# Second-order attention on one NeuronCore: the waits of a visit's state products, the bank of every other output mix, and one residual's place

## The chip, the cores and the metric

The kernel runs on one core of a Trainium2 chip. The metric is the time of one execution on the device in microseconds (us), the median of several runs. The profile is one execution taken by the hardware profiler; its rows give the busy time of TensorE (PE, with PEld for its weight loads), VectorE (DVE), ScalarE (ACT) and GpSimd (POOL).

## What is computed

Eight layers run one behind the other on an input of 8 x 1024 rows of 256 numbers, each as x = x + layer(layernorm(x)). The change touches the fifth, a second-order linear attention with 16 heads of 32 dimensions. The reference, cut to that layer:

```python
def step(carry, qkv):
    S_K, C_QV, G = carry
    q_t, k_t, v_t = qkv
    C_prev = GAMMA * C_QV
    k_C = jnp.einsum('bhk,bhkv->bhv', k_t, C_prev)
    G = GAMMA * G + k_t[..., :, None] * k_C[..., None, :]
    S_K = GAMMA * S_K + k_t[..., :, None] * k_t[..., None, :]
    C_QV = C_prev + q_t[..., :, None] * v_t[..., None, :]
    S_C = jnp.einsum('bhij,bhjv->bhiv', S_K, C_QV)
    o_t = jnp.einsum('bhk,bhkv->bhv', q_t, S_C - G)
    return ((S_K, C_QV, G), o_t)
_, outs = jax.lax.scan(step, (S_K0, C_QV0, G0), (q, k, v))
out = outs.transpose(1, 0, 2, 3).reshape(Bs, Ts, H * DV)
return out @ Wo
```

GAMMA is 0.99; q, k and v are x @ Wq, x @ Wk and x @ Wv.

## The kernel before

All layers are written by hand: each engine has its own program, in a fixed order, and waits on semaphores for the others. The layer in question is the function second_order_attention. It works in chunks: the 8192 rows are 64 tiles of 128 rows (NT = 64), eight tiles to a batch (TB = 8). The 16 heads are four groups of four (HG = 4, UT = 4), and a **visit** t is one tile with one group: t runs over 256 visits (NU), tile(t) = t // 4. Every group carries three 32x32 states per head from tile to tile of its batch. A visit *carries* a state (carries(t)) unless its tile is the first of its batch, and updates it unless its tile is the last.

PE's loop over t runs from L1792 of the listing on. One turn of it does, in this order:

- keys_queries(t) (L1651), the products of keys and queries of the chunk, into the four banks so_rows, and queries_U(t-1) (L1659). DVE masks the first (mask_AB, L1962) and the second (mask_P, L1970) into AB and PT.
- turn_KQ(t) and turn_W(t-1) (L1672, L1673, L1666), transposes into bank U. ACT copies them out as KW and KQe (L1885, L1891, L1892).
- a **filler**, which has nothing to do with the visit's own heads: by t % 8 it is a projection of v (0 and 1, L1708), of q or k (3 to 6, L1688), or a **mix**, the product with Wo of a finished tile (L1719). mixes_at(t) puts the mix of an even tile m at t = 4m + 7, so t % 8 = 7, and that of an odd tile at t % 8 = 2, followed there by turn_x (L1681), the transpose of the next tile pair's normalised x into bank J.
- the products of the visit: state_to_UW(t) (L1734 into bank U, L1737 into bank C), state_to_O(t-1) (L1743 and L1746 into bank X), keys_to_U(t) (L1752), values_to_W(t) (L1759), values_to_O(t-1) (L1766, L1769), state_products(t-1) (L1776, L1779, bank X).

Four PSUM banks are shared: U, C, X and J. Bank X holds the mix in its first 256 columns, the state updates and O behind them. Bank J holds the projections and turn_x, each copied out by ACT (copy_turned, copy_V, copy_xT) and for x also read by DVE (low_xT, L1936).

The state products work on 32x32 tiles of the array. Head h of the four sits on row group h, and its column group differs:

```python
nc.tensor.matmul(bU[head_rows(h), 0:P], state_of(t, 0, h), QTg[head_rows(h), tile(t) % 2, t % UT],
                 start=True, stop=False, tile_position=(h * DK, h * DK))
nc.tensor.matmul(bC[turned_rows(h), 0:P], state_of(t, 2, h), KTg[head_rows(h), tile(t) % 2, t % UT],
                 start=True, stop=False, tile_position=(h * DK, (h + 1) % HG * DK))
nc.tensor.matmul(bX[crossed_rows(h), O_AT], state_of(t, 2, h), Ug[head_rows(h), t % 2],
                 start=True, stop=False, tile_position=(h * DK, (h + 2) % HG * DK))
```

DVE's turn t: copy_O(t-2) (L1956), update(t-2) (L1946, L1948), mask_AB(t), mask_P(t-1), at t % 8 = 2 low_xT, then residual(m) for a mix of this turn (L1975: X = X + bank X, which also increments x_ready), and statistics of the rows one turn later (L1979). POOL multiplies by the decay (QTg, KTg, Ug) and makes the low part of O (L2041). PE waits for x_ready before anything in a visit writes bank X again.

Of the kernel before, what the change touches and what calls it, by code (L numbers as in the profile page):

```python
# [21 lines left out]
NT = BATCH * TB  # L22
# [1521 lines left out]
def second_order_attention(nc, R, A, C, joined):  # L1544
# [6 lines left out]
    with Stage(nc, "so") as st:  # L1551
# [46 lines left out]
        def mixes_to(t):  # L1598
            return sum(len(mixes_at(n)) for n in range(t + 1))
# [22 lines left out]
        with joined.stack:  # L1622
# [16 lines left out]
            def _(pe):  # L1639
# [62 lines left out]
                def project_V(i):  # L1702
                    if i % 2 == 0:
                        pe.wait_ge(s_["KT_ready"], halves_to(i))
                    else:
                        pe.wait_ge(s_["V_ready"], i)
# [5 lines left out]
                def mix(i, t):  # L1712
                    pe.wait_ge(s_["O_ready"], UT * (i + 1))
                    pe.wait_ge(s_["S_ready"], updates_to(min(t - 2, NU - 1)))
                    pe.wait_ge(s_["O_copied"], min(t - 1, NU))
                    if i >= 1:
                        pe.wait_ge(s_["x_ready"], i)
                    for m, (a, b, u) in enumerate((a, b, u) for a, b in PARTS for u in range(UT)):
                        last = nc.tensor.matmul(bX[:, 0:HID], OT[:, a, (UT * i + u) % (2 * UT)], wo[:, b, u],  # L1719
                                                start=(m == 0), stop=(m == UT * len(PARTS) - 1))  # L1720
# [8 lines left out]
                def state_to_UW(t):  # L1729
                    pe.wait_ge(s_["S_ready"], updates_to(t - UT))  # L1730
                    pe.wait_ge(s_["QTg_ready"], carrying_tiles_to(tile(t)))
                    pe.wait_ge(s_["KTg_ready"], carrying_tiles_to(tile(t)))
# [7 lines left out]
                def state_to_O(t):  # L1740
                    pe.wait_ge(s_["Ug_ready"], carries_to(t))
                    for h in range(HG):
                        nc.tensor.matmul(bX[crossed_rows(h), O_AT], state_of(t, 2, h), Ug[head_rows(h), t % 2],  # L1743
                                         start=True, stop=False, tile_position=(h * DK, (h + 2) % HG * DK))
                    for h in range(HG):
# [46 lines left out]
                for t in range(NU + 3):  # L1792
# [25 lines left out]
                    if t < NU and carries(t):  # L1818
                        state_to_UW(t)
                    if 2 <= t <= NU:  # L1820
                        pe.wait_ge(s_["O_copied"], t - 1)
                        pe.wait_ge(s_["S_ready"], updates_to(t - 2))
                        if mixes_to(t) >= 1:
                            pe.wait_ge(s_["x_ready"], mixes_to(t))
                    if 1 <= t <= NU and carries(t - 1):
                        state_to_O(t - 1)
# [97 lines left out]
            def _(dve):  # L1924
# [48 lines left out]
                def residual(i):  # L1973
                    dve.wait_ge(s_["out_done"], i + 1)
                    nc.vector.tensor_tensor(R.X[:, i, :], R.X[:, i, :], bX[:, 0:HID], ALU.add).then_inc(s_["x_ready"], 1)  # L1975
# [9 lines left out]
                for t in range(NU + 4):  # L1985
# [14 lines left out]
                    if t == STATS_AT + NT // 2 + 2:  # L2000
                        dve.wait_ge(s_["std_ready"], 2)
                        scales(nc, c, R, REST)
                        nc.vector.memset(R.turnstile[:], 0.0).then_inc(s_["scaled"], 1)
                    if 1 <= t <= NU:
# [3 lines left out]
                    for m in mixes_at(t):  # L2008
                        residual(m)
# [1210 lines left out]
```

## Time and profile before

| | us |
|---|---|
| median of 3 runs (lowest, highest) | 3633.62 (3632.8, 3638.25) |
| the profiled execution's own time | 3635.29 |
| its span in the profile | 3633.3 |
| the loop over the visits, from 1523.6 to 2812.95 | 1289.4 |

The profile's timeline rows begin with the start of a group of instructions and how long it lasted, both in us; then engine, line, operation, what is written and read, the shape, and the count. PE splits an f32 product in two passes, each with a weight load, so four products are eight rows' worth (x8), and where two groups interleave they show as x4 and x4. A bracket at the end gives the idle time of the engine before the row and who ended it. The end of a product is modelled, so in PE's rows the starts are what counts.

### The profile page before, as it was taken

Reading aid. Unit: us, or ns where it says so; the run is one execution under the profiler, and the core shown is the slowest. Engines: PE = TensorE matmul, PEld = TensorE weight load, DVE = VectorE, ACT = ScalarE, POOL = GpSimd, SP = SyncE. Lnnn points to the kernel's source line nnn. Section 1 sums busy time; section 2 is a strip of 40 time slices with the busy share of each in tenths; the row PEclk is TensorE's granted clock in tenths of the full one; section 3 lists DMA queues with packets and bytes.
Section 4 is the critical chain, followed back from the end, with each engine's and each line's share of the span. In section 5 each row is a group of like instructions: output and inputs, shape, how many; then the busy total and the mean of one; then the engine's idle time right before and its main releaser. Section 6 shows DMA issues by size and latency. Waiting matters only on the chain. (4 is left out here: it accounts for less than half of the span.)

```text
span 3633.3 us, 137840 instructions
## 1 busy us (share of the span) xinstructions
PE 3322.4 (91%) x55606; PEld 2924.4 (80%) x55606; DVE 2265.3 (62%) x6633; ACT 2046.7 (56%) x6370; POOL 1377.9 (38%) x2094
## 2 busy tenths in 40 slices
PE   8939999799948999899999999999999999999998
PEld 8929999777737999787888887887887778888877
DVE  6675555688874555555544544444545688888887
ACT  5546565455445565433434443433443689999996
POOL 5755565201024665232323223232322633333225
PEclk9969999999978999999999999999999999999999
DMA  4153342511144443500000000000000133343332
GB/s 128 48 171 81 87 96 55 158 48 54 48 154 118 97 94 64 137 3 3 4 3 4 3 3 3 4 4 3 3 3 4 44 101 115 114 125 107 104 96 98
DMA packets 202924, 235.36 MB, mean 65 GB/s; under 512 B 17968, under 2 KB 182976, under 8 KB 202304
## 3 DMA queue, kind: packets, MB, share of 16 engines
q1 hardware_dynamic: 177728, 192.99, 16.9%
q0 software_dynamic: 24576, 33.57, 5.4%
q8 instruction: 454, 7.44, 0.9%
q14 instruction: 166, 1.36, 0.1%
HBM read 147.46 MB, written 79.04 MB: 62 GB/s over the span
## 5 line engine op out<-in xcount | busy, mean ns | idle before, releaser
L2502 ACT ACTIVATE wa_S<-wa_S,wa_top 128x192 f32<-128x192 f32 x1024 | 463.0, 476 | 36.7 <-DVE wa_top L2598 36.7
L2041 POOL TENSOR_TENSOR so_OT<-so_O,so_OT 128x128 fp32r<-128x128 f32 x256 | 117.6, 459 | 763.4 <-ACT so_OT L1877 763.4
L1956 DVE COPY so_O<-so_bankX 128x128 f32<-128x128 f32 x256 | 74.7, 292 | 507.3 <-PE so_bankX L1769 449.7
L1962 DVE TENSOR_TENSOR so_raw<-so_rows,so_masks 128x1024 f32<-128x1024 f32 x256 | 313.6, 1225 | 109.2 <-PE so_rows L1659 101.4
L2598 DVE CUSTOM_DVE_ANT_0 wa_S<-wa_bank,wa_band 128x192 f32<-128x192 f32 x1024 | 295.1, 349 | 3.4 <-issue 3.4
L1885 ACT ACTIVATE so_KW<-so_bankU 128x128 f32<-128x128 f32 x256 | 71.2, 278 | 326.1 <-PE so_bankU L1666 326.1
L650 POOL DMA_INDIRECT sum_dram<-y,rows x128 | 223.5, 1746 | 29.4 <-issue 26.8
L2390 PE MATMUL wa_bank<-ident,wa_S 128*128 128x128 f32 x1536 | 221.2, 277 | 7.7 <-ACT wa_probT L2509 4.7
L2502 ACT ACTIVATION_READ_ACCUMULATOR wa_S<-wa_S,wa_top 128x1 f32 x1024 | 224.0, 219 | 0.0
L1688 PE MATMUL so_bankJ<-so_xnT,so_w 128*128 128x256 f32 x1500 | 211.8, 291 | 6.7 <-DVE so_xnT L1936 6.6
L728 ACT ACTIVATE m2e_hT<-m_bank,m2e_bias 128x256 fp32r<-128x256 f32 x256 | 126.7, 495 | 154.3 <-PE m_bank L680 148.4
L728 ACT ACTIVATE m4e_hT<-m_bank,m4e_bias 128x256 fp32r<-128x256 f32 x256 | 126.4, 494 | 148.8 <-PE m_bank L680 142.5
L2390 PEld LDWEIGHTS wa_bank<-ident,wa_S 128*128 128x128 f32 x1536 | 172.7, 140 | 36.6 <-ACT wa_S L2502 16.8
L1688 PEld LDWEIGHTS so_bankJ<-so_xnT,so_w 128*128 128x128 f32 x1500 | 188.9, 191 | 7.6 <-DVE so_xnT L1936 6.9
L680 PE MATMUL m_bank<-m2e_exT,m_w_parts 128*128 128x256 f32 x1536 | 191.3, 285 | 0.0
L680 PE MATMUL m_bank<-m4e_exT,m_w_parts 128*128 128x256 f32 x1536 | 189.6, 283 | 0.0
L694 PE MATMUL m_bank<-m_w_parts,m4e_hT 128*128 128x256 f32 x1536 | 187.0, 281 | 0.6 <-DVE m4e_pre L775 0.6
L694 PE MATMUL m_bank<-m_w_parts,m2e_hT 128*128 128x256 f32 x1536 | 187.0, 281 | 0.6 <-DVE m2e_pre L775 0.6
L680 PEld LDWEIGHTS m_bank<-m2e_exT,m_w_parts 128*128 128x128 f32 x1536 | 185.7, 192 | 0.0
L694 PEld LDWEIGHTS m_bank<-m_w_parts,m2e_hT 128*128 128x128 f32 x1536 | 184.0, 188 | 0.8 <-issue 0.8
L694 PEld LDWEIGHTS m_bank<-m_w_parts,m4e_hT 128*128 128x128 f32 x1536 | 184.0, 188 | 0.8 <-issue 0.8
L680 PEld LDWEIGHTS m_bank<-m4e_exT,m_w_parts 128*128 128x128 f32 x1536 | 184.0, 190 | 0.0
(456 smaller groups left out, 9758.2 us busy)
## 6 DMA issues: line engine op xcount, KB each, us to landing
m_w_raw<-in_L_ffn_W_dram SPq DMA_DIRECT2D x64, 512.0 KB
wa_V<-wa_V_dram SPq DMA_DIRECT2D x256, 128.0 KB, 2.8
sum_dram<-X SPq DMA_DIRECT2D x16, 1024.0 KB, 4.6
X<-sum_dram SPq DMA_DIRECT2D x16, 1024.0 KB, 7.6
wa_V_dram<-wa_V_new SPq DMA_DIRECT2D x32, 512.0 KB, 3.6
wa_V_rest<-wa_V_dram SPq DMA_DIRECT2D x128, 128.0 KB, 3.1
X<-in_L_attn_a_x_dram SPq DMA_DIRECT2D x8, 1024.0 KB, 11.5
xn_dram<-m2r_xn SPq DMA_DIRECT2D x16, 512.0 KB, 4.5
```

Source lines behind the costliest of these rows:

```text
L650: nc.gpsimd.indirect_dma_start(out=summed, out_offset=bass.IndirectOffsetOnAxis(ap=rows[:, s, u:u + 1], axis=0), in_=y[:, s % 2, u, :], in ...
L680: last = nc.tensor.matmul(bank[:, 0:2 * P], w_parts[:, par, a, c, f * P:(f + 1) * P], exT[:, s % 2, b, c], start=(n == 0), stop=(n == len( ...
L694: last = nc.tensor.matmul(by[u][:, 0:HID], hT[:, s % 2, a, f, u * P:(u + 1) * P], w_parts[:, par, b, 2 + f // QF, f % QF * HID:(f % QF + 1 ...
L728: last = nc.scalar.activation(to, bh[f % 4][:, 0:2 * P], ACT.Gelu_apprx_tanh, bias=bias[:, par, f:f + 1])
L1688: last = nc.tensor.matmul(bank[:, 2 * k * P:2 * (k + 1) * P], w[:, a, n, c, cols], xnT[:, b, c], start=(m == 0), stop=(m == 2 * len(PARTS) ...
L1885: nc.scalar.mul(KW[:, t % 2, 1], bU[:, 3 * P:4 * P], -1.0).then_inc(s_["W_ready"], 1)
L1956: nc.vector.tensor_copy(O[:, t % UT], bX[:, O_AT]).then_inc(s_["O_copied"], 1)
L1962: nc.vector.tensor_tensor(AB[:, t % 2].rearrange("p h m t -> p h (m t)"), rows4[:, :, 0:2 * P], masks[:].rearrange("p m t -> p (m t)")[:, ...
L2041: nc.gpsimd.tensor_tensor(OT[:, 1, t % (2 * UT)], O[:, t % UT], OT[:, 0, t % (2 * UT)].bitcast(F32), ALU.subtract).then_inc(s_["O_ready"], 1)
L2390: last = nc.tensor.transpose(to[:, h * P:(h + 1) * P], of, R.ident[:])
L2502: nc.scalar.activation(S[:, n % 2, z], S[:, n % 2, z], ACT.Exp, bias=top[:, n % 2, z:z + 1], scale=-1.0, accum_out=sums[:, i % 2, SET * c ...
L2598: nc.vector.tensor_tensor_reduce(out=S[:, n % 2, z], in0=bS[g][:, eo * SPAN:(eo + 1) * SPAN], in1=band[:], scale=-(D ** -0.5), scalar=3e38 ...
```

## The change

1. PE, state products of a visit. All waits now stand ahead of the first tile: those for U and W (W_ready, K_ready, KQe_ready, QTg_ready, KTg_ready) and those for O (O_copied, S_ready, x_ready, Ug_ready). state_to_O is split in updates_to_O and queries_to_O, which have no waits.
2. The mix of an even tile goes to bank J (bJ) in place of bank X. mix, project_V and the visit's x_ready wait are adapted: the visit waits only for the residuals of mixes in bank X.
3. DVE: the residual of an odd tile's mix (bank X) stands ahead of mask_P; that of an even tile's stays behind it.

```diff
+        def mixed(m):
+            return bX if m % 2 else bJ
+
+        def mixes_in_states_to(t):
+            return sum(m % 2 for n in range(t + 1) for m in mixes_at(n))
...
                     if i % 2 == 0:
                         pe.wait_ge(s_["KT_ready"], halves_to(i))
+                        if i >= 2:
+                            pe.wait_ge(s_["x_ready"], i - 1)
...
                 def mix(i, t):
                     pe.wait_ge(s_["O_ready"], UT * (i + 1))
-                    pe.wait_ge(s_["S_ready"], updates_to(min(t - 2, NU - 1)))
-                    pe.wait_ge(s_["O_copied"], min(t - 1, NU))
-                    if i >= 1:
-                        pe.wait_ge(s_["x_ready"], i)
+                    if i % 2:
+                        pe.wait_ge(s_["S_ready"], updates_to(min(t - 2, NU - 1)))
+                        pe.wait_ge(s_["O_copied"], min(t - 1, NU))
+                    elif i + 2 < NT:
+                        pe.wait_ge(s_["KT_ready"], halves_to(i + 2))
+                    else:
+                        pe.wait_ge(s_["V_ready"], NT)
...
-                        last = nc.tensor.matmul(bX[:, 0:HID], OT[:, a, (UT * i + u) % (2 * UT)], wo[:, b, u],
+                        last = nc.tensor.matmul(mixed(i)[:, 0:HID], OT[:, a, (UT * i + u) % (2 * UT)], wo[:, b, u],
...
                 def state_to_UW(t):
-                    pe.wait_ge(s_["S_ready"], updates_to(t - UT))
-                    pe.wait_ge(s_["QTg_ready"], carrying_tiles_to(tile(t)))
-                    pe.wait_ge(s_["KTg_ready"], carrying_tiles_to(tile(t)))
...
-                def state_to_O(t):
-                    pe.wait_ge(s_["Ug_ready"], carries_to(t))
+                def updates_to_O(t):
...
+                def queries_to_O(t):
...
-                    if t < NU and carries(t):
-                        state_to_UW(t)
                     if 2 <= t <= NU:
                         pe.wait_ge(s_["O_copied"], t - 1)
                         pe.wait_ge(s_["S_ready"], updates_to(t - 2))
-                        if mixes_to(t) >= 1:
-                            pe.wait_ge(s_["x_ready"], mixes_to(t))
+                        if mixes_in_states_to(t) >= 1:
+                            pe.wait_ge(s_["x_ready"], 2 * mixes_in_states_to(t))
+                    if t < NU and carries(t):
+                        pe.wait_ge(s_["QTg_ready"], carrying_tiles_to(tile(t)))
+                        pe.wait_ge(s_["KTg_ready"], carrying_tiles_to(tile(t)))
                     if 1 <= t <= NU and carries(t - 1):
-                        state_to_O(t - 1)
+                        pe.wait_ge(s_["Ug_ready"], carries_to(t - 1))
+                    if t < NU and carries(t):
+                        state_to_UW(t)
+                    if 1 <= t <= NU and carries(t - 1):
+                        updates_to_O(t - 1)
+                        queries_to_O(t - 1)
...
                 def residual(i):
                     dve.wait_ge(s_["out_done"], i + 1)
-                    nc.vector.tensor_tensor(R.X[:, i, :], R.X[:, i, :], bX[:, 0:HID], ALU.add).then_inc(s_["x_ready"], 1)
+                    nc.vector.tensor_tensor(R.X[:, i, :], R.X[:, i, :], mixed(i)[:, 0:HID], ALU.add).then_inc(s_["x_ready"], 1)
...
+                    for m in mixes_at(t):
+                        if mixed(m) is bX:
+                            residual(m)
                     if 1 <= t <= NU:
                         mask_P(t - 1)
                     if t % (2 * UT) == 2 and tile(t) + 2 < NT:
                         low_xT(tile(t) // 2 + 1)
                     for m in mixes_at(t):
-                        residual(m)
+                        if mixed(m) is bJ:
+                            residual(m)
```

The order of instructions on PE, at the products of a visit with an odd mix, before. Semaphores are reused from earlier layers, and the listing gives them the names of their first owners: sp_k_done is S_ready, la_pT_ready O_copied, sp_XL_ready x_ready, sp_shifted Ug_ready, la_share_ready QTg_ready, la_x_ready KTg_ready, la_before_ready KQe_ready, la_xT_low K_ready and sp_k_ready W_ready.

```order
L1719 MATMUL so_bankX<-so_wo,so_OT 128x256 x11
L1681 MATMUL so_bankJ<-ident,so_xn 128x128 [waits la_v_done,m2_w_high]
L1681 MATMUL so_bankJ<-ident,so_xn 128x128 x3
L1734 MATMUL so_bankU<-so_QTg,so_state 32x128 [waits sp_k_done,la_share_ready,la_before_ready,la_x_ready,la_xT_low,sp_k_ready]
L1734 MATMUL so_bankU<-so_QTg,so_state 32x128 x3
L1737 MATMUL so_bankC<-so_KTg,so_state 32x128 x4
L1743 MATMUL so_bankX<-so_Ug,so_state 32x128 [waits sp_XL_ready,sp_shifted,sp_k_done,la_pT_ready]
L1743 MATMUL so_bankX<-so_Ug,so_state 32x128 x3
L1746 MATMUL so_bankX<-so_QTg,so_state 32x128 x4
L1752 MATMUL so_bankU<-so_raw,so_KW 32x128 [waits la_cleared]
```

And now, the same place:

```order
L1727 MATMUL so_bankX<-so_wo,so_OT 128x256 x11
L1684 MATMUL so_bankJ<-ident,so_xn 128x128 [waits la_v_done,m2_w_high]
L1684 MATMUL so_bankJ<-ident,so_xn 128x128 x3
L1739 MATMUL so_bankU<-so_QTg,so_state 32x128 [waits sp_XL_ready,sp_k_done,la_share_ready,la_pT_ready,la_x_ready,la_before_ready,sp_shifted,la_xT_low,sp_k_ready]
L1739 MATMUL so_bankU<-so_QTg,so_state 32x128 x3
L1742 MATMUL so_bankC<-so_KTg,so_state 32x128 x4
L1747 MATMUL so_bankX<-so_Ug,so_state 32x128 x4
L1752 MATMUL so_bankX<-so_QTg,so_state 32x128 x4
L1758 MATMUL so_bankU<-so_raw,so_KW 32x128 [waits la_cleared]
```

The products stand in the same order; the waits of the third group moved to the first, which has nine in place of six, and the third group has none. (Line numbers of the changed kernel are up to 16 higher: L1752 there is the second half of O, and keys_to_U is L1758.)

DVE, the turn with an odd mix, before:

```order
L1956 COPY so_O<-so_bankX 128x128
L1946 SCALAR_TENSOR_TENSOR so_state<-so_state,so_bankX 128x96
L1962 TENSOR_TENSOR so_raw<-so_rows,so_masks 128x1024
L1970 TENSOR_TENSOR so_raw<-so_rows,so_masks 128x512
L1936 TENSOR_TENSOR so_xnT<-so_bankJ,so_xnT 128x512
L1975 TENSOR_TENSOR X<-X,so_bankX 128x256
```

And now:

```order
L1968 COPY so_O<-so_bankX 128x128
L1958 SCALAR_TENSOR_TENSOR so_state<-so_state,so_bankX 128x96
L1974 TENSOR_TENSOR so_raw<-so_rows,so_masks 128x1024
L1987 TENSOR_TENSOR X<-X,so_bankX 128x256
L1982 TENSOR_TENSOR so_raw<-so_rows,so_masks 128x512
L1948 TENSOR_TENSOR so_xnT<-so_bankJ,so_xnT 128x512
```

The residual moved past mask_P and low_xT.

## Rows read from the trace of the kernel before

**Rows 1.** The page of the kernel before, part 1: engine, busy us (share of the span), xinstructions

```profile
PE 3322.4 (91%) x55606; PEld 2924.4 (80%) x55606; DVE 2265.3 (62%) x6633; ACT 2046.7 (56%) x6370; POOL 1377.9 (38%) x2094
```

**Rows 2.** Windows: the stage, then one undisturbed round of eight visits

```profile
core 0: us, PE busy (x) PEld busy (x) DVE busy (x) ACT busy (x) POOL busy (x), PEclk, DMA share, GB/s
1523.60:2812.95 1289.35, 1214.67 (x30221) 1038.60 (x30216) 650.51 (x1182) 517.72 (x1742) 386.59 (x647) 1.00 0.01 3
1925.60:1966.60 41.00, 39.11 (x1023) 33.66 (x1008) 20.40 (x37) 16.43 (x55) 13.33 (x23) 1.00 0.02 4
```

**Rows 3.** Who PE waited for in the stage: us, times, longest

```profile
PE so_bankX L1743 <- DVE X L1975: 47.2, 55, 1.6
PE so_bankU L1752 <- DVE X L1975: 13.5, 7, 1.9
PE so_rows L1659 <- issue: 5.8, 9, 1.1
```

**Rows 4.** Timeline of PE, plain visit: start us, us, engine, line, out<-in, count [idle]

```profile
2404.22 0.28 PE L1688 MATMUL so_bankJ<-so_xnT,so_w 128*128 128x256 f32 x1
2404.43 0.31 PE L1734 MATMUL so_bankU<-so_QTg,so_state 32*32 32x128 f32 x4
2404.46 0.31 PE L1737 MATMUL so_bankC<-so_KTg,so_state 32*32 32x128 f32 x4
2404.57 0.29 PE L1734 MATMUL so_bankU<-so_QTg,so_state 32*32 32x128 f32 x4
...
2404.67 0.42 PE L1743 MATMUL so_bankX<-so_Ug,so_state 32*32 32x128 f32 x8
...
2405.24 0.32 PE L1752 MATMUL so_bankU<-so_raw,so_KW 128*32 128x128 f32 x4
```

**Rows 5.** Timeline of PE's weight loads, the same plain visit

```profile
2404.49 0.12 PEld L1737 LDWEIGHTS so_bankC<-so_KTg,so_state 32*32 32x32 f32 x4
2404.64 0.18 PEld L1743 LDWEIGHTS so_bankX<-so_Ug,so_state 32*32 32x32 f32 x8
```

**Rows 6.** Timeline of all engines, visit with an even mix

```profile
2407.62 1.67 PE L1719 MATMUL so_bankX<-so_wo,so_OT 128*128 128x256 f32 x12
...
2409.22 0.31 PE L1734 MATMUL so_bankU<-so_QTg,so_state 32*32 32x128 f32 x4
...
2409.33 0.42 DVE L1975 TENSOR_TENSOR X<-X,so_bankX 128x256 f32<-128x256 f32 x1
...
2410.01 0.42 PE L1743 MATMUL so_bankX<-so_Ug,so_state 32*32 32x128 f32 x8 [0.34 <-DVE X L1975]
...
2410.57 0.32 PE L1752 MATMUL so_bankU<-so_raw,so_KW 128*32 128x128 f32 x4
```

**Rows 7.** Timeline of all engines, visit with an odd mix that carries a state

```profile
2381.48 1.67 PE L1719 MATMUL so_bankX<-so_wo,so_OT 128*128 128x256 f32 x12
...
2382.45 0.68 DVE L1970 TENSOR_TENSOR so_raw<-so_rows,so_masks 128x512 f32<-128x512 f32 x1
...
2383.51 0.31 PE L1734 MATMUL so_bankU<-so_QTg,so_state 32*32 32x128 f32 x4
...
2384.24 0.69 DVE L1936 TENSOR_TENSOR so_xnT<-so_bankJ,so_xnT 128x512 fp32r<-128x512 f32 x1 [1.10 <-ACT so_xnT L1847]
...
2384.85 0.41 DVE L1975 TENSOR_TENSOR X<-X,so_bankX 128x256 f32<-128x256 f32 x1
...
2385.51 0.42 PE L1743 MATMUL so_bankX<-so_Ug,so_state 32*32 32x128 f32 x8 [1.55 <-DVE X L1975]
...
2386.08 0.32 PE L1752 MATMUL so_bankU<-so_raw,so_KW 128*32 128x128 f32 x4
```

**Rows 8.** Timeline of PE, visit with an odd mix, no state carried

```profile
1858.62 0.43 PE L1752 MATMUL so_bankU<-so_raw,so_KW 128*32 128x128 f32 x8 [1.93 <-DVE X L1975]
```

**Rows 9.** Timeline of ACT, end of the copies ahead of a plain visit

```profile
2403.43 0.49 ACT L1892 ACTIVATE so_KQe<-so_bankU,so_to_end 128x256 f32<-128x256 f32 x1
```

**Rows 10.** DMA queues in the stage: transfers, MB, share of 16 engines

```profile
q8 instruction: 244, 4.00, 1.3%
```

More of the change, by code:

```diff
@@ L1596, in mixes_at @@
             return [m for m in (2 * ((t - 7) // 8), 2 * ((t - 10) // 8) + 1) if 0 <= m < NT and t == 8 * (m // 2) + (7, 10)[m % 2]]
-        def mixes_to(t):
-            return sum(len(mixes_at(n)) for n in range(t + 1))
+        def mixed(m):
+            return bX if m % 2 else bJ
+        def mixes_in_states_to(t):
+            return sum(m % 2 for n in range(t + 1) for m in mixes_at(n))
         def halves_to(i):
```

## The prediction

> **What bounds the kernel now.** The page's part 1 comes first: PE is busy 91% of the span, DVE 62%, ACT 56% [rows 1]. [...] An undisturbed round of eight visits takes 41.0 us, PE 39.1 of them [rows 2]. So PE sets the pace, and a gain must be idle or badly packed PE time. The view of who waited for whom then names the idle part: 47.2 us in 55 waits of the state's products into bank X, and 13.5 us in 7 waits of the keys' product, all for DVE's residual, L1975 [rows 3]. With PE's instruction feed (5.8 us in nine, "issue") that is nearly all of its idle time. Last, the timelines of three kinds of visit show where those waits lie and how PE packs its small tiles [rows 4 to 8].
>
> A visit has four stretches on PE: rows, turns, a filler (projection, mix or turn) and the state products. Wherever keys_to_U (L1752) starts earlier, U, W, O, the masks of the next visit and all the rest start earlier by the same time, since each waits for PE's end of a product. I therefore measure each kind of visit from its state products to L1752.
>
> **How many of each.** Of 256 visits, 28 in each batch of 32 carry a state, and 27 of these follow a visit that does: 216 have U/W products and O products together. Even mixes fall at t % 8 = 7, always in such a visit: 32. Odd mixes fall at t % 8 = 2: 31 inside the loop, 24 that carry and 7 in the first tile of a batch that don't (the 55 and 7 of [rows 3] agree, one record missing). Plain ones: 216 - 32 - 24 = 160.
>
> **Part 1, the waits ahead of the first tile.** In a plain visit the U loads begin at 2404.43, those of W right behind at 2404.46 (as its products do), and the last W loads at 2404.49; then nothing loads until 2404.64, where the O group starts; its products start at 2404.67 and L1752 at 2405.24 [rows 4, 5]. The O group sits behind its own waits, all long satisfied. U, W and O lie on three different sets of 32x32 tiles (row h, columns h, h+1, h+2), and W's first products start 0.03 us after U's, while U's second passes (2404.57) come later still. So a group on free tiles is taken at once. With no wait between, O should follow W as W follows U, at about 2404.49: 0.15 earlier by the load, 0.18 by the product, which now starts 0.03 behind its load. I take 0.17. Bounds: at best 0.19; at least 0.05, if O can only start behind the second W passes (from 2404.59); nothing or less if the third set cannot run beside the others. 160 x 0.17 = 27.2 us.
>
> What is moved in front: the waits for O_copied, S_ready, x_ready and Ug_ready. What they cost there is hidden: the last copy the visit waits for ends at 2403.92 [rows 9], the last projection product starts at 2404.22 and holds the tiles to 2404.43 [rows 4], so the queue of waits has 0.5 us of cover. If it were gone, one more pair of waits is worth up to 0.1 us (0.15 is the whole gap of the waits that stand between W and O now). The copy of O and the state update are the first things DVE does in a visit, and Ug follows the copy of U, ahead of the turns and the filler; none of them is late.
>
> [...] First the row: W's loads and products begin 0.03 us behind U's, while U's products run, on the same four row groups, and U's second passes start after W's first [rows 4]. [...]
>
> **Part 2, even mixes in the projections' bank.** The mix ends at 2409.29, the residual runs 2409.33 to 2409.75, and O starts at 2410.01, 0.79 us after U at 2409.22 [rows 6]; in a plain visit it is 0.24 [rows 4]. In bank J nobody in the state products waits for the residual: 0.55 back, and part 1's 0.17 with it: 0.72 x 32 = 23.0 us. Bank J is free then: the last projection was copied in the visit before, and the next user, project_V, comes one visit later. Its added wait costs nothing.
>
> **Part 3, odd mixes, the residual ahead of mask_P.** Today DVE does mask_P (2382.45 to 2383.13), waits for ACT's copy of the turned x, does low_xT (2384.24), and only then the residual: 2384.85 to 2385.26. O starts 0.25 behind, at 2385.51, L1752 at 2386.08 [rows 7]. The mix ended at 2383.15. With the residual first it runs 2383.19 to 2383.60, 1.66 us sooner. All state products now wait for it. Behind the residual stands PE's queue of waits: 0.25 us as now, or more, since more waits stand behind x_ready; with three pairs instead of one I take 0.45. U, W and O start at 2384.05, and L1752 follows 0.81 - 0.17 = 0.64 later, at 2384.69: 1.39, say 1.40 us sooner. 1.40 x 24 = 33.6 us (1.60 each if it stays 0.25). mask_P slips to 2383.60-2384.28; its reader, values_to_O, comes after L1752's 2384.69, so this costs nothing, and low_xT still ends at about 2384.97, a visit before it is read.
> The 7 without a state wait 1.93 us at L1752 [rows 8]; the same 1.66 less 0.1 for the queue: 1.55 x 7 = 10.9 us.
>
> **The sum.** 27.2 + 23.0 + 33.6 + 10.9 = 94.7 us. The profiled execution took 3635.3 us, 2.0 more than its span and 1.7 more than the median of the three runs. 3635.3 - 94.7 = 3540.6; on the median's scale 3538.9. I forecast **3540 us**, 2.6% less. A measurement of this kernel tells some 0.2% (7 us) from no change.
>
> **The rivals.**
> *O cannot overlap W and U* (25%). Then a visit gains 0.05, not 0.17: 216 x 0.12 = 26 us less, 3566. [...] Against: U beside W.
> *Instructions come late* (12%). PE already starves nine times at L1659, 0.6 us each, 1.1 at most [rows 3], and its code arrives in 244 transfers, 4 MB, over the stage [rows 10]. The waits for the residual were time in which the feed caught up. With the stage 7% shorter some 20 to 60 more gaps of 0.6 us would give back 12 to 36 us: 3552 to 3576.
> *The waits in front show* (6%). They might be worked off only when the filler drains: 0.1 x 216 = 22 us back, 3562. This is also how the change would fail to do what it says: the wait is moved, not hidden.
> *Slower, by the feed* (3%). If PE's demand passes what the feed delivers, most of the 244 transfers are waited for. The gain is eaten at 94.7 / 0.64 = 148 gaps (5.8 us / 9 = 0.64 each); if all 244 cost the longest, 1.1 us, that is 268 - 6 = 262 more: 3540 + 262 = 3802; at 0.64 each 3690. Against: nine of 244 now, while whole rounds run at 41.0 us without one.
>
> **How the numbers follow.** The forecast case, everything within a few us of the sum, has 52%; the four rivals 46%; 2% is left for a change with no effect, since bank X may be waited for where I don't see it. The low end: 0.19 in place of 0.17 (4 us), 1.60 for 1.40 (5 us), the feed gaps gone (6 us), some 5 more from an undisturbed clock: 3540 - 20 = 3520. The high end: no overlap (26) and a few more gaps (14): 3580. Chances: faster by over 0.2% 0.94, within 0.02, slower 0.04.
>
> **What would show it.** An undisturbed round of eight should take 41.0 - 6 x 0.17 - 0.72 - 1.40 = 37.9 us. In a plain visit O's first loads should start within 0.07 us of U's and L1752 0.64 behind U, not 0.81. After an even mix the same 0.64, and no wait for the residual; after an odd one U, W and O together, 0.25 to 0.5 behind the residual, and L1752 about 1.5 us after the mix ends. The waits for the residual should fall from 61 us to under 12. I am wrong if U starts later in plain visits (waits exposed), if O still starts 0.2 behind U (no overlap), or if "issue" before L1659 grows from 6 us to tens.

## The result, and the profile after

| | before | after |
|---|---|---|
| median of the runs (lowest, highest), us | 3633.65 (3632.8, 3638.25) | 3535.1 (3529.74, 3535.58) |
| the profiled execution's own time, us | 3635.29 | 3529.74 |
| its span, us | 3633.3 | 3527.8 |

The ratio is 0.9723, with an interval from 0.9706 to 0.974, from four runs of each: 98.6 us less by the medians. The forecast was 3540, 94.7 less than before.

The page's part 1 of the changed kernel, where [rows 1] stood before:

```profile
PE 3262.7 (92%) x55606; PEld 2885.2 (82%) x55606; DVE 2266.3 (64%) x6633; ACT 2043.5 (58%) x6370; POOL 1375.0 (39%) x2094
```

The counts of products and weight loads are what they were. Semaphore instructions are not in them: the traces have 3622 of PE's before, of which 1326 hold two waits and the others one, and 3368 after, of which 1505 hold two. There are fewer since S_ready was waited for in both groups, and since more waits stand side by side and share an instruction. Of the 55606 weight loads 5059 carry a wait before and 4843 after, none more than one. The windows view of the changed kernel, over the loop and over one undisturbed round of eight visits, as [rows 2] (length of the window, then busy time and count of each engine, the granted clock, the share of the DMA engines and what they moved):

```profile
1523.60:2709.60 1186.00, 1159.49 (x30225) 1002.70 (x30220) 652.96 (x1182) 516.21 (x1742) 385.87 (x647) 1.00 0.01 4
2148.20:2185.90 37.70, 37.21 (x1014) 32.41 (x1008) 20.39 (x37) 16.43 (x55) 13.25 (x23) 1.00 0.02 4
```

The loop is 103 us shorter and holds all but 2 us of the 105.6 between the two profiled executions. PE, idle 1.9 us in a round of 41.0 before, is idle 0.5 us in a round of 37.7. Who PE waited for in the loop of the changed kernel, as [rows 3] (waiting line, who ended the wait, us in total, times, the longest):

```profile
PE so_bankU L1739 <- DVE X L1987: 12.2, 24, 0.9
PE so_rows L1654 <- issue: 5.0, 7, 1.1
PE so_bankU L1739 <- ACT so_KW L1903: 4.2, 4, 1.1
PE so_bankU L1758 <- DVE X L1987: 1.9, 7, 0.3
```

The residual was waited for 60.7 us in 62 waits, and is now for 14.1 us in 31: the 24 odd mixes of visits that carry, and the 7 that don't.

**A plain visit.** PE's timeline of the changed kernel, as [rows 4] (start, duration, engine, line, operation, tile, shape, count):

```profile
2165.72 0.31 PE L1739 MATMUL so_bankU<-so_QTg,so_state 32*32 32x128 f32 x4
2165.74 0.31 PE L1742 MATMUL so_bankC<-so_KTg,so_state 32*32 32x128 f32 x4
2165.77 0.31 PE L1747 MATMUL so_bankX<-so_Ug,so_state 32*32 32x128 f32 x4
2165.85 0.29 PE L1739 MATMUL so_bankU<-so_QTg,so_state 32*32 32x128 f32 x4
2165.88 0.29 PE L1742 MATMUL so_bankC<-so_KTg,so_state 32*32 32x128 f32 x4
2165.90 0.29 PE L1747 MATMUL so_bankX<-so_Ug,so_state 32*32 32x128 f32 x4
...
2166.01 0.40 PE L1752 MATMUL so_bankX<-so_QTg,so_state 32*32 32x128 f32 x8
2166.34 0.16 PEld L1758 LDWEIGHTS so_bankU<-so_raw,so_KW 128*32 128x32 f32 x8 [0.20 <-issue]
2166.34 0.42 PE L1758 MATMUL so_bankU<-so_raw,so_KW 128*32 128x128 f32 x8
```

Two passes to a product can be counted here: a group of the state products has four in the program, and in the trace eight records of PE and eight loads, x4 and x4 at L1739 (2165.72 and 2165.85), L1742 and L1747, x8 at L1752. It does not hold for every product that the rows call f32: the 12 of a mix stand as x12 [rows 6, 7].

U, W and O begin 0.02 to 0.03 apart, and their second passes follow in the same order. The keys' product (L1752 before, L1758 now) begins 0.62 behind U, where it was 0.81. Its loads, where O stood 0.15 us behind W in [rows 5]:

```profile
2165.76 0.10 PEld L1742 LDWEIGHTS so_bankC<-so_KTg,so_state 32*32 32x32 f32 x1
2165.76 0.10 PEld L1739 LDWEIGHTS so_bankU<-so_QTg,so_state 32*32 32x32 f32 x1
2165.77 0.10 PEld L1747 LDWEIGHTS so_bankX<-so_Ug,so_state 32*32 32x32 f32 x1
2165.77 0.10 PEld L1742 LDWEIGHTS so_bankC<-so_KTg,so_state 32*32 32x32 f32 x1
```

O's first weights are loaded between those of W's and U's passes. **After an even mix** it is the same picture, and the residual (L1987, from bank J) runs beside the state products, where O waited for it in [rows 6]:

```profile
2184.12 0.31 PE L1739 MATMUL so_bankU<-so_QTg,so_state 32*32 32x128 f32 x4
...
2184.17 0.31 PE L1747 MATMUL so_bankX<-so_Ug,so_state 32*32 32x128 f32 x4
...
2184.22 0.42 DVE L1987 TENSOR_TENSOR X<-X,so_bankJ 128x256 f32<-128x256 f32 x1
...
2184.74 0.42 PE L1758 MATMUL so_bankU<-so_raw,so_KW 128*32 128x128 f32 x8
```

**After an odd mix**, as [rows 7], the residual runs as soon as the mix is done, and all state products start behind it:

```profile
2196.25 1.67 PE L1727 MATMUL so_bankX<-so_wo,so_OT 128*128 128x256 f32 x12
...
2197.96 0.42 DVE L1987 TENSOR_TENSOR X<-X,so_bankX 128x256 f32<-128x256 f32 x1 [0.65 <-PE so_bankX L1727]
2198.30 0.68 DVE L1982 TENSOR_TENSOR so_raw<-so_rows,so_masks 128x512 f32<-128x512 f32 x1
...
2198.85 0.31 PE L1739 MATMUL so_bankU<-so_QTg,so_state 32*32 32x128 f32 x4 [0.48 <-DVE X L1987]
...
2199.48 0.42 PE L1758 MATMUL so_bankU<-so_raw,so_KW 128*32 128x128 f32 x8
```

The residual ends at 2198.38, U starts 0.47 later, and the keys' product 1.56 behind the mix's end (2197.92). What fills the 0.47 us stands in the trace too: four semaphore instructions of PE, at 2198.42, 2198.53, 2198.64 and 2198.74, 0.106 us apart. They hold eight of the nine waits; the ninth is carried by U's first load, at 2198.82. The wait for the residual is in the first of the four.

**A measure for all kernels.** The rest of the text uses one count made from each trace: the time from the first row product of a visit to that of the next. The eight batches repeat the same 32 visits. The *undisturbed* time of a visit is the third shortest of the eight at its place in the batch (its own time where that is shorter, as in the last pair of tiles), and their sum over the loop is what the loop takes without accidents; the loop's real time less that sum is its *excess*. The columns plain, even mix and odd mix give the time to which the undisturbed visits of a kind come back, most of them within 0.02 us. Gaps are idle times of PE over 0.45 us in the loop, ahead of an instruction that waits for nothing (the view's "issue").

| kernel | plain | even mix | odd mix | round of 8 | loop | undisturbed | excess | gaps |
|---|---|---|---|---|---|---|---|---|
| before | 4.79 | 5.34 | 6.99 | 41.0 | 1292.8 | 1271.3 | 21.5 | 8 |
| after | 4.605 | 4.605 | 5.61 | 37.75 | 1189.5 | 1175.5 | 14.0 | 9 |

Odd mixes of a first tile, which carry no state, went from 6.42 to 4.77.

### The profile page after: what moved, and what is told of

It reads as the page before. It is cut to its first block and busy times, and to the rows that moved or that the text cites. A ratio compares the mean times of both kernels' runs of the same rounds, so it can differ in the third digit from the quotient of the medians.

```text
span 3527.8 us, 137586 instructions
## 1 busy us (share of the span) xinstructions
PE 3262.7 (92%) x55606; PEld 2885.2 (82%) x55606; DVE 2266.3 (64%) x6633; ACT 2043.5 (58%) x6370; POOL 1375.0 (39%) x2094
## 5 line engine op out<-in xcount | busy, mean ns | idle before, releaser
L1974 DVE TENSOR_TENSOR so_raw<-so_rows,so_masks 128x1024 f32<-128x1024 f32 x256 | 313.4, 1224 | 105.8 <-PE so_rows L1662 98.6
L2406 PEld LDWEIGHTS wa_bank<-ident,wa_S 128*128 128x128 f32 x1536 | 172.6, 140 | 36.5 <-ACT wa_S L2518 16.9
```

What stands on the lines that cost most here:

```text
L1974: nc.vector.tensor_tensor(AB[:, t % 2].rearrange("p h m t -> p h (m t)"), rows4[:, :, 0:2 * P], masks[:].rearrange("p m t -> p (m t)")[:, ...
L2406: last = nc.tensor.transpose(to[:, h * P:(h + 1) * P], of, R.ident[:])
```

## The experiments

### The three parts alone, and the change without its first part

The waits alone: the kernel before, with every wait of the visit ahead of its first tile.

```diff
-                    if t < NU and carries(t):
-                        state_to_UW(t)
...
+                    if t < NU and carries(t):
+                        pe.wait_ge(s_["QTg_ready"], carrying_tiles_to(tile(t)))
+                        pe.wait_ge(s_["KTg_ready"], carrying_tiles_to(tile(t)))
+                    if 1 <= t <= NU and carries(t - 1):
+                        pe.wait_ge(s_["Ug_ready"], carries_to(t - 1))
+                    if t < NU and carries(t):
+                        state_to_UW(t)
                     if 1 <= t <= NU and carries(t - 1):
                         state_to_O(t - 1)
```

> Part 1 alone: all waits of a visit's state products ahead of the first tile, every mix still in bank X, every residual still last on DVE. Theory (the third set of tiles packs beside the other two once no wait stands between; the change gained 0.187 us in each plain visit): 160 plain visits x 0.187 = 29.9 us less. But now U and W wait for the residual too: after it come 0.44 us of waits and 0.66 us of state products to the keys' product, 1.10, where before it was 0.25 + 0.57 = 0.82 (2385.26 to 2386.08): 0.28 more in each of the 32 visits with an even mix and the 24 odd ones with a state, 15.7 us. Sum 14 us less, 3619 us. Rival (the gain is the wait instructions' own time, so it comes in every visit): 216 x 0.187 = 40 us less, 3593. Rival (moving waits gives nothing without the other parts): 3633 or more.

The even mixes in bank J alone: the change, with the waits back at their places and all residuals behind the masks.

```diff
-                    for m in mixes_at(t):
-                        if mixed(m) is bX:
-                            residual(m)
...
+                    if t < NU and carries(t):
...
+                        state_to_UW(t)
                     if 2 <= t <= NU:
                         pe.wait_ge(s_["O_copied"], t - 1)
```

> Part 2 alone: even mixes in bank J, waits in the middle as before, residuals last on DVE as before. Theory: each of 32 visits loses its wait for the residual, 0.55 us: 17.6 us less, 3616 us, rounds of eight visits 41.0 - 0.55 = 40.45 us. Rival (bank J is not free, the projection behind waits): under 10 us less, with new waits of PE before the projection of v.

The residual alone: the kernel before, with the residual of an odd tile ahead of mask_P.

```diff
+                    for m in mixes_at(t):
+                        if m % 2:
+                            residual(m)
                     if 1 <= t <= NU:
                         mask_P(t - 1)
```

> Part 3 alone: the residual of odd mixes ahead of mask_P, everything else as before. Theory: the residual ends 1.66 us sooner in 31 visits, and only the O group waits for it, with 0.25 us behind it as before: 31 x 1.66 = 51 us less, 3582 us; rounds of eight 41.0 - 1.66 = 39.3 us. Rival (mask_P, now behind, is late for the product that reads it): less than 40 us gained, with PE waiting for L1970's mask in these visits.

The second and third part together: the change, with the waits back at their places.

```diff
+                    if t < NU and carries(t):
...
+                        state_to_UW(t)
                     if 2 <= t <= NU:
                         pe.wait_ge(s_["O_copied"], t - 1)
...
                     if 1 <= t <= NU and carries(t - 1):
                         pe.wait_ge(s_["Ug_ready"], carries_to(t - 1))
-                    if t < NU and carries(t):
-                        state_to_UW(t)
-                    if 1 <= t <= NU and carries(t - 1):
```

> Parts 2 and 3 without part 1 (the waits of the O group stand between W and O). Theory: the two parts add up, 17.6 + 51 = 69 us less than before, 3565 us, 30 more than the change: part 1 is worth 192 visits x 0.187 = 36 us in the visits without a wait for a residual and costs 0.28 x 24 = 7 in the odd ones. A plain visit takes 4.79 us, as before. Rival (part 1 is worth little once the others stand): within 10 us of 3535.

| kernel | median (ratio, interval) | plain | even mix | odd mix | round of 8 | undisturbed | excess | gaps |
|---|---|---|---|---|---|---|---|---|
| waits alone | 3642.2 (1.0023, 1.0006 to 1.0039) | 4.605 | 5.61 | 7.26 | 40.48 | 1257.2 | 46.5 | 17 |
| bank alone | 3620.7 (0.9963, 0.9949 to 0.9977) | 4.79 | 4.79 | 6.99 | 40.43 | 1253.8 | 23.0 | 13 |
| residual alone | 3595.0 (0.9889, 0.9872 to 0.9905) | 4.79 | 5.34 | 5.34 | 39.32 | 1221.4 | 36.5 | 22 |
| bank and residual | 3576.5 (0.984, 0.9823 to 0.9856) | 4.79 | 4.79 | 5.34 | 38.79 | 1204.5 | 31.8 | 21 |

Each part does in its own visits what the prediction's steps say, and leaves the others alone. The bank takes 0.55 from even mixes, the residual 1.65 from odd ones. The waits take 0.185 from each of six plain visits and *add* 0.27 at either mix, where U and W, which used to run ahead of the residual's wait, now stand behind it. The rows of the waits-alone kernel say it (who PE waited for, in the loop):

```profile
PE so_bankU L1731 <- DVE X L1976: 81.7, 56, 2.2
PE so_bankU L1748 <- DVE X L1976: 13.5, 7, 1.9
PE so_rows L1651 <- issue: 8.2, 10, 1.1
```

The waits alone are the surprise. Their undisturbed loop is 14 us shorter than before, just as was expected, but the median is 9 us longer than that of the kernel before on the same chip (3633.3): the excess is 46.5 us in place of 21.5. A part of that is the clock. Two windows of that kernel side by side, and the wait between them:

```profile
2416.40:2424.00 7.60, 7.60 (x185) 6.04 (x182) 4.88 (x9) 3.33 (x12) 1.54 (x4) 1.00 0.02 4
2424.00:2434.00 10.00, 7.86 (x214) 6.75 (x195) 3.29 (x6) 2.99 (x10) 3.51 (x6) 0.85 0.02 4
```

```profile
2430.96 0.43 PE L1731 MATMUL so_bankU<-so_QTg,so_state 32*32 32x128 f32 x4 [2.14 <-DVE X L1976]
2430.99 0.44 PE L1734 MATMUL so_bankC<-so_KTg,so_state 32*32 32x128 f32 x4
```

After PE has stood still for 2.14 us at this place the granted clock is 0.50 (from 2431.10 to 2434.30 in the windows view; 1.00 from 2435 to 2438), and a group of products that takes 0.31 us takes 0.43. The trace has 11 such stretches in this loop, each 3.4 us long; this one makes its visit 8.69 us long in place of 7.26. At 1.4 us each they are about 16 us in all. They don't follow every such wait: the loop has 30 waits of 1.9 to 2.2 us for an odd mix's residual, and 19 of them are not followed by one. The kernel before has 2, behind two of its seven waits of 1.9 us [rows 8], and the bank alone none behind the same seven. The change has none in either of its two profiles, and PE no idle time over 1.3 us. So nine stretches more than before cost some 13 of the 25 us of excess, and the idle time in gaps, 13.9 us in place of 5.9, another 8; the rest is open. By its median the first part loses a little without the other two, and the order in which the parts are applied decides what one sees of it.

The other three kernels are 5 to 13 us above what was expected of them, though their rounds are as reckoned (40.43, 39.32, 38.79). In the two with the residual that rest lies in the excess, 15 and 10 us more than before, and there mostly in the gaps (11 and 10 us more), taken up below. The bank's profiled execution is 17 us shorter than the one before, as expected; only its median (13) is not. For the kernel without the waits, who PE waited for:

```profile
PE so_rows L1654 <- issue: 8.3, 12, 1.3
PE so_rows L1662 <- issue: 7.2, 10, 1.2
PE so_bankU L1739 <- ACT so_KW L1902: 4.3, 4, 1.1
PE so_bankU L1758 <- DVE X L1986: 1.9, 7, 0.3
```

Its residual costs odd visits nothing at all by this view: U and W fill the time that the residual needs. In the change they don't, and the odd visit is 5.61 against 5.34. On top of the other two parts, the first gives 0.185 seven times a round and takes 0.27 once.

### One wait and two between W and O

The change, with the wait for Ug back between W and O; and with a wait for O_copied there too (the one ahead of U stays).

```diff
                     if 1 <= t <= NU and carries(t - 1):
+                        pe.wait_ge(s_["Ug_ready"], carries_to(t - 1))
                         updates_to_O(t - 1)
```

> The change, with one of the moved waits (Ug_ready, long satisfied) back between W and O. A round of eight undisturbed visits takes 37.8 us with none there and 41.0 - 0.55 - 1.66 = 38.8 with four. Theory A (what costs is the time to work off the queue of waits that stands between; a single wait rides on the weight load itself): O starts at most 0.05 us later than with none, 37.8 to 38.2 us a round, under 10 us in all. Theory B (any wait there ends the packing of the third set): the full 0.187 back in a visit, 39.2 us a round, about 3535 + 40 = 3575 us.

```diff
                         pe.wait_ge(s_["Ug_ready"], carries_to(t - 1))
+                        if t >= 2:
+                            pe.wait_ge(s_["O_copied"], t - 1)
                         updates_to_O(t - 1)
```

> The change, with two of the moved waits (Ug_ready, O_copied) back between W and O. Theory A (queue of waits, one rides on the load, the other is worked off ahead of it): about 0.1 us more in each of 216 visits than the change, 38.6 us a round, 3535 + 22 = 3557 us. Theory B (packing lost with the first wait): as with one, 39.2 us a round. Theory C (each wait costs a quarter of 0.187): 0.09 for two, 0.05 for one.

One wait: 3529.1 us (0.9726, 0.9709 to 0.9744), plain visit 4.61, odd mix 5.50, round 37.66. Two waits: 3556.9 us (0.9786, 0.977 to 0.9803), plain visit 4.68, round 38.3. With the kernel that has four waits there (4.79), a plain visit costs 0, 0.075 and 0.185 more for one, two and four waits. PE's weight loads in a plain visit of the kernel with one wait, and of that with two:

```profile
1790.92 0.12 PEld L1739 LDWEIGHTS so_bankU<-so_QTg,so_state 32*32 32x32 f32 x4
...
1790.98 0.10 PEld L1747 LDWEIGHTS so_bankX<-so_Ug,so_state 32*32 32x32 f32 x1
```

```profile
1799.14 0.12 PEld L1739 LDWEIGHTS so_bankU<-so_QTg,so_state 32*32 32x32 f32 x4
...
1799.20 0.12 PEld L1742 LDWEIGHTS so_bankC<-so_KTg,so_state 32*32 32x32 f32 x4
1799.24 0.18 PEld L1747 LDWEIGHTS so_bankX<-so_Ug,so_state 32*32 32x32 f32 x8
```

With one satisfied wait O's first load begins 0.053 us behind U's in the trace, as in the change with none; with two O's loads come in one block, 0.10 behind U's first, and with four 0.21 behind [rows 4, 5]. In the traces of the kernels with one, two and four waits O's first load carries one of them itself, and the others are semaphore instructions of their own: with one wait there is none of these between W and O, with two there is one, which holds one wait (at 1799.17), and with four there are two, which hold one and two (at 2404.45 and 2404.56 in the kernel before). In these kernels the visit so became longer only with the waits beyond the one on the load. The odd mix's 5.50 fits this: with Ug's wait gone from the front, three semaphore instructions stand there in place of four, again 0.106 us apart, and the visit is 0.11 shorter. The prediction took all four waits as the gap and didn't tell which of them make it.

### O first, and the wait for the residual first

In the change O's chain is the longest of the three, since queries_to_O follows updates_to_O on the same tiles (L1747 from 2165.77, L1752 from 2166.01, while U's and W's last passes start by 2165.90). Here it starts first:

```diff
                     if 1 <= t <= NU and carries(t - 1):
                         pe.wait_ge(s_["Ug_ready"], carries_to(t - 1))
+                        updates_to_O(t - 1)
                     if t < NU and carries(t):
                         state_to_UW(t)
                     if 1 <= t <= NU and carries(t - 1):
-                        updates_to_O(t - 1)
                         queries_to_O(t - 1)
```

> The change, with the order updates_to_O, U, W, queries_to_O: O's two groups lie on the same tiles and take four passes one behind the other, the longest chain, and now start 0.053 us before U instead of behind W. Theory (three sets of tiles run beside each other, so the chain on O's tiles sets the length): 0.053 us less in each of 216 visits, 11 us, 3524 us, rounds of 37.8 - 0.4 = 37.4. Rival (PE takes the groups in program order, so O's second group behind U and W starts as late as now): no change.

And here the wait for the residual, the only late one, stands first of the visit's waits, so that the long satisfied ones are no longer queued behind it:

```diff
+                    if 2 <= t <= NU and mixes_in_states_to(t) >= 1:
+                        pe.wait_ge(s_["x_ready"], 2 * mixes_in_states_to(t))
                     if 1 <= t <= NU:
                         pe.wait_ge(s_["W_ready"], t)
```

> The change, with x_ready named first of the visit's waits, which puts it on the first weight load itself, with no wait behind it; before, three pairs of waits were worked off behind it (0.44 us from the residual's end to the U group). Theory: in an odd visit U starts 0.1 to 0.15 behind the residual, 0.3 us less, in 31 visits: 9 us, 3526 us; the odd visit takes 5.3 in place of 5.6 us. Rival (the 0.44 is the time for a semaphore to arrive): no change.

The timeline of the kernel with O first:

```profile
1794.31 0.31 PE L1747 MATMUL so_bankX<-so_Ug,so_state 32*32 32x128 f32 x4
1794.33 0.31 PE L1739 MATMUL so_bankU<-so_QTg,so_state 32*32 32x128 f32 x4
1794.36 0.31 PE L1742 MATMUL so_bankC<-so_KTg,so_state 32*32 32x128 f32 x4
...
1794.55 0.40 PE L1752 MATMUL so_bankX<-so_QTg,so_state 32*32 32x128 f32 x8
1794.87 0.43 PE L1758 MATMUL so_bankU<-so_raw,so_KW 128*32 128x128 f32 x8
```

The keys' product is 0.56 behind the first tile, not 0.62, and a plain visit takes 4.55. The three sets of tiles begin 0.02 to 0.03 us apart in either order. With the residual's wait first:

```profile
1787.38 0.42 DVE L1987 TENSOR_TENSOR X<-X,so_bankX 128x256 f32<-128x256 f32 x1 [0.65 <-PE so_bankX L1727]
...
1787.86 0.31 PE L1739 MATMUL so_bankU<-so_QTg,so_state 32*32 32x128 f32 x4
```

U's first load carries the wait for the residual itself, and no semaphore instruction of PE stands between the residual's end and that load. U starts 0.06 us behind the residual's end (1787.80), not 0.47, and the odd mix's visit takes 5.20, not 5.61. Both rounds shrink as they should, to about 37.4. But the medians are 3534.5 (0.9728, 0.9711 to 0.9744) and 3536.9 (0.974, 0.9724 to 0.9757): nothing against the change's own 3535.1, where 3524 and 3526 were expected. Their undisturbed loops are 11 and 9 us shorter (1164.6, 1166.2), their excess is 32 and 30 us in place of 14, with 20 gaps each in place of 9. Is that the price of a denser visit, or an accident of the change's profiled execution? Three kernels on one chip answer.

### The change again, both together, and 64 instructions more

The change unaltered; the two edits above together; and the change with 16 more warm-up products, 64 PE instructions, ahead of the loop (its page has 55638 products and as many loads, 32 more of each):

```diff
-                for _ in range(30):
+                for _ in range(46):
                     nc.tensor.matmul(bC[:, 0:P], R.ident[:], R.ident[:], start=True, stop=True)
```

> The change once more, beside the next two on the same chip, so that differences of a few us can be read. 3535 us, rounds of 37.8.

> O's first group ahead of U and W, and x_ready on the first load. Undisturbed rounds of eight: 37.8 - 0.35 - 0.3 = 37.15 us, 20 us less over the loop than the change if PE's instruction feed costs the same. The two edits alone took 0.3 us off a round and gave nothing in the median, while gaps without a wait took 10 us more in their profiles. Theory (the feed takes what the visits give): 3525 to 3535, gaps again in visits 71 to 83 and 168 to 178. Rival (the medians were chance): 3515.

> The change, with 16 more warm-up products on PE ahead of the loop (30 to 46), which are 64 more instructions: all of PE's later code lies 64 instructions further in its blocks of 256. In every profile so far each gap of PE that no wait explains (over 0.45 us) lies a multiple of 256 PE instructions behind the one before, in the first 60 instructions of a visit. Theory (PE's code arrives in blocks of 256, and only a border in this stretch, where PE takes small products fastest, is felt): borders now fall there in visits 8 to 26, 103 to 119 and 198 to 214, so gaps are found in these and none in 66 to 95 or 165 to 178; undisturbed rounds 37.8 as before; total within 15 us of 3535, rather above, since 66 visits in place of 52 have such a border. Rival (gaps come by place in the program or by time): in visits 71 to 83 and 168 to 178 as before.

| kernel | median (lowest, highest) | ratio to before | undisturbed | excess | gaps |
|---|---|---|---|---|---|
| the change again | 3537.0 (3521.1, 3547.7) | 0.9725 (0.970 to 0.975) | 1175.8 | 33.0 | 19 |
| both together | 3527.3 (3522.0, 3532.5) | 0.971 (0.9696 to 0.9723) | 1154.3 | 33.3 | 22 |
| 64 instructions more | 3559.9 (3547.8, 3570.0) | 0.979 (0.9774 to 0.9807) | 1178.2 | 43.9 | 32 |

The change again settles the question: the same program has 19 gaps in this profile and 9 in its first, and its own runs spread over 27 us. Dense visits are not needed for it. The gaps are not the whole of the excess: that is 19 us larger than in the first profile, the idle time in gaps 8 us (14.8 against 6.4). Which gaps there are, the two timelines show (in brackets the idle time ahead). The change again has these between 1855 and 1885 us, and none between 1595 and 1628:

```profile
1862.64 0.37 PE L1662 MATMUL so_rows<-so_U,so_QT 32*128 32x128 f32 x1 [0.68 <-issue]
...
1869.50 0.26 PE L1654 MATMUL so_rows<-so_KT,so_QT 32*128 32x128 f32 x1 [1.11 <-issue]
...
1880.31 0.39 PE L1654 MATMUL so_rows<-so_KT,so_QT 32*128 32x128 f32 x3 [0.56 <-issue]
```

With 64 more instructions it is the other way round:

```profile
1598.72 0.26 PE L1654 MATMUL so_rows<-so_KT,so_QT 32*128 32x128 f32 x1 [0.54 <-issue]
...
1604.26 0.50 PE L1662 MATMUL so_rows<-so_U,so_QT 32*128 32x128 f32 x7 [0.51 <-issue]
```

Counted in the traces (products, loads and semaphore instructions), the gaps of every kernel lie a multiple of 256 PE instructions apart, to within three. That the code comes in blocks of this size is inferred from the counts: the loop of the kernel before has 62650 PE instructions and 244 transfers in the instruction queue [rows 10], the change's has 62399 and 243, 257 to a transfer in both. Most plain visits have 261 to 263 instructions, so that a border of 256 drifts slowly through the visits, and the gaps came where it falls among the first 60 or so instructions of one, the row products (L1654, L1662) and the transposes behind them. Two gaps of the thirteen profiles lie elsewhere, among a visit's last products: one of the waits alone (visit 79), one of the residual alone (visit 109). In the change again the gaps are at visits 71 to 84 and 167 to 178. Had the borders' place nothing to do with it, 64 more instructions would have changed nothing; they moved the gaps to visits 15 to 26, 107 to 122 and 207 to 215, and removed both old clusters. They also cost 23 us by the medians, where at most 15 was expected. In the profiled pair the difference is 22 us, of which 13 lie in the loop, where three clusters fit in place of two; 5 lie ahead of the added products, where the edit changes nothing.

Both edits together give 9.7 us over the change again on the same chip, and every one of their five runs is below the change's median. The intervals of the two ratios overlap, so that this is the best version found, but only likely a faster one. Its round is 36.92.

## Why the prediction was right

*The count and the local terms.* They hold one by one, in the undisturbed visits: plain 0.185 against 0.17, even mix 0.735 against 0.72, odd mix 1.38 against 1.40, first tile's odd mix 1.65 against 1.55. With the prediction's counts: 160 x 0.185 + 32 x 0.735 + 24 x 1.38 + 7 x 1.65 = 97.8 us (94.7 were forecast). The undisturbed loops differ by 95.8, the medians by 98.6. The profiled pair differs by 105.6: its excess also fell, from 21.5 to 14.0 us, which the change again (33.0) shows to be the luck of that execution. The local terms are right by their mechanism; that the total came within 5 us of the forecast is in part luck, since the same visits take 3559.9 us with 64 instructions more ahead of them, and nothing in the sum stands for where the borders fall.

*The signs to look for.* Round 37.9: 37.75. O's loads within 0.07 of U's: 0.05 (2165.77 against 2165.72). The keys' product 0.64 behind U: 0.62. U 0.25 to 0.5 behind the residual: 0.47, against the 0.45 taken. Waits for the residual under 12 us: 14.1, a small miss. The 24 waits at U average 0.51 us, and each holds the residual's own 0.42 and the queue behind it, less the cover of the filler (turn_x).

*O cannot overlap W and U* is refuted by three kernels: the changed one, the one with a single wait and the one with O first. Its 25% was the author's estimate. In these traces all three sets lie on the same four row groups and start 0.03 us apart, and O's first products (2165.77) come ahead of the second passes of U's products (2165.85), which stand before O in the program.

*The waits in front show*: not in plain visits, whose gain is at the upper bound. In visits with an odd mix they do, 0.41 us each, as the kernel with the residual's wait first shows; the prediction had 0.45 of it in its sum, for "three pairs" of waits where the trace has four instructions. It didn't see that the order of the waits could take it away. It did say that all state products of an odd mix wait for the residual; that the same holds at an even mix while that is in bank X, and that the first part alone gains nothing by the median, it didn't say.

*Instructions come late* was half right. The gaps exist, number 8 to 32 in a loop, and hold 6 to 23 us of idle time; but they don't follow from the shorter stage. The kernels with the bank or the residual alone, 13 and 38 us shorter than before, have 13 and 22, and the change, shorter than both, has 9 in one execution and 19 in another. At which visits they can be goes with where the borders of 256 instructions fall, as 64 instructions more showed (visits 15 to 26 in place of 71 to 84). What decides whether a cluster is there in an execution is open: no run here tells it. *Slower by the feed* didn't come.

*The parts don't add by their medians*: -9, 13 and 38 alone make 42, and together they are 98.6. By undisturbed loops the waits gain 14.1 alone and 29.0 on top of the other two, the bank 17.5 and the residual 49.9. The 15 us between 14.1 and 29.0 are the 32 even mixes, where the waits cost 0.27 alone and give 0.185 once the bank is changed. The rest of the first part's 41.4 us by the medians (3576.5 to 3535.1) isn't its own work: the excess beside it fell by 18 in the change's first profile, and rose by 1 in its second.

## What to carry to other kernels

Measure an edit in undisturbed visits as well as by the median: here the one is good to 0.02 us a visit, while the other moves by 10 to 25 us with the gaps at the borders of 256 instructions (one program gave 3521.1 to 3547.7). Here three groups of products on three sets of tiles began 0.02 to 0.03 us apart when no wait or one stood ahead of the third (plain visit 4.605 and 4.61), and the third came 0.10 and 0.21 us behind the first with two and four (4.68 and 4.79). So try satisfied waits ahead of the first group, or a single one at the next, and name the wait that ends last first: that took the odd mix's visit from 5.61 to 5.20. A part that gains nothing alone by the median may still be worth its gain beside others: the waits alone lost 9 us by the median and took 14.1 off the undisturbed loop, and 29.0 once the other two parts stood.

## What was not expected of the hardware

- **Borders of 256 PE instructions.** Idle times of 0.5 to 1.5 us with nothing waited for, a multiple of 256 instructions from one another; the queue of [rows 10] brings 4.00 MB in 244 transfers, so 16 KB each, and the loop has 257 PE instructions to one of them. With 243 or 244 transfers to a loop 8 to 32 gaps were found; those hold 6 to 23 us of idle time in loops of 1188 to 1304, nearly all where the border falls among the small products at the start of a visit.
- **The clock.** A wait of about 2 us in an otherwise busy stretch was followed by 3.4 us at a granted clock of 0.50, in place of 1.00, in 11 of 30 cases in one loop (the waits alone): 1.4 us more for the visit, on top of the wait. None of the shorter ones in the change's two profiles, up to 1.3 us, was.
- **Satisfied waits.** In every trace of this case no weight load carries more than one wait and no semaphore instruction of PE more than two; the four behind a residual stood 0.106 us apart. One wait between W and O cost a plain visit nothing (4.61 against 4.605), two 0.075 us (4.68), four 0.185 (4.79). With four instructions from the late wait on U started 0.47 us behind the residual, with none 0.06.
